# Attention scores on 32-row tiles of TensorE, the mask of the exponentials on GpSimd, and the last two batches out of the loop

## The reference, cut to what matters

```python
k = (x @ Wk).reshape(b, t, h, s)          # b, t, h, s = 8, 512, 16, 8
q = (x @ Wq).reshape(b, t, h, s)
v = (x @ Wv).reshape(b, t, h, s)
k = _layernorm(k, kln_w, kln_b)
q = _layernorm(q, qln_w, qln_b)
dot = jnp.einsum('bqhs,bkhs->bhqk', q, k) * scale
dot = jnp.where(causal, dot, -jnp.inf)
attn = jax.nn.softmax(dot, axis=-1)
out = jnp.einsum('bhqk,bkhs->bqhs', attn, v).reshape(b, t, e)
return out @ Wo + bo
```

## Time and profile before

| | |
|---|---|
| three executions, us | 1347.28, 1348.21, 1350.85; median 1348.21 |
| profiled execution | 1348.36 us, its span 1346.3 us |
| mean granted TensorE clock | 0.907 of full speed |
| busy share of the span | PE 78%, weight loads 53%, DVE 65%, ACT 44%, POOL 31% |
| chain that ended last | PE 40%, DVE 17%, issue 12% |

### The profile page before, as it was taken

One profiled execution on the slowest core, in us unless ns is written; L12 is line 12 of the kernel. 1 busy time (PEld: TensorE's weight loads), 2 busy tenths in 40 slices (PEclk: granted clock), 3 DMA queues, 4 the chain that ended last, 5 costly groups with the idle time before them and its releaser, 6 DMA issues.

```text
span 1346.3 us, 22600 instructions
## 1 busy us (share of the span) xinstructions
PE 1055.1 (78%) x6332; PEld 711.3 (53%) x6332; DVE 871.3 (65%) x1881; ACT 594.5 (44%) x1109; POOL 417.8 (31%) x460
## 2 busy tenths in 40 slices
PE   7699999879898989989898778877776321499970
PEld 4355544765555656656565454444444321399960
DVE  6677741247686777778677647999996555244445
ACT  6555554125464555555465555454454101144420
POOL 4100000771412124031000023355352177266660
PEclk9899999989998999999899989899998555699995
DMA  4011113321000000000000195000001011223206
GB/s 116 32 63 62 62 62 125 128 84 25 17 25 16 19 19 23 17 17 24 18 22 19 33 156 134 1 0 0 0 0 31 6 52 34 68 79 89 96 27 186
DMA packets 64911, 66.80 MB, mean 50 GB/s; under 512 B 7842, under 2 KB 53356, under 8 KB 62800
## 3 DMA queue, kind: packets, MB, share of 16 engines
q1 hardware_dynamic: 50256, 54.52, 14.9%
q0 software_dynamic: 4608, 6.61, 1.6%
q10 hardware_dynamic: 9984, 4.80, 1.3%
HBM read 29.90 MB, written 29.43 MB: 44 GB/s over the span
## 4 chain that ended last, share of the span: by engine, by line
PE 40%; DVE 17%; issue 12%; ACT 3%; POOL 2%; DMA 2%; DVEq 1%; POOLq 0%; ACTq 0%; SPq 0%
PE banks L1739 6%; PE banks L1753 6%; PE banks L1767 6%; PE banks L1799 5%; PE banks L2000 5%; PE banks L1992 4%; DVE D_gun L1123 2%; PE banks L1741 2%; DVE D_dmx L1079 2%; POOL rows_dram L776 2%; DVE B_mneg L951 1%; DVE D_sc L1110 1%; DMA F_back<-y_dram 1%; PE banks L1840 1%; ACT B_ot L1435 1%
## 5 line engine op out<-in xcount | busy, mean ns | idle before, releaser
L951 DVE TENSOR_REDUCE B_mneg<-banks 128x2 f32<-128x256 f32 (+3 forms) x273 | 223.9, 822 | 110.3 <-PE banks L1741 104.0
L1429 ACT ACTIVATE B_pt<-banks 128x1024 f32<-128x1024 f32 (+3 forms) x260 | 181.6, 708 | 146.2 <-PE banks L1753 144.8
L1739 PE MATMUL banks<-B_kp,B_qt 128*128 128x128 f32 (+3 forms) x546 | 181.4, 393 | 4.2 <-DMA B_kp<-B_kt 2.3
L1753 PE MATMUL banks<-B_qt,B_kp 128*128 128x512 f32 (+3 forms) x520 | 146.3, 363 | 13.3 <-issue 7.7
L1739 PEld LDWEIGHTS banks<-B_kp,B_qt 128*128 128x128 f32 x546 | 109.4, 201 | 62.9 <-ACT B_pt L1429 43.7
L1741 PE MATMUL banks<-B_mask_q,B_identb 128*128 128x128 bf16 x546 | 125.1, 234 | 0.0
L793 POOL DMA_INDIRECT y_dram<-F_yo,F_ide x80 | 80.7, 1009 | 67.0 <-DVE F_yo L1277 42.9
L1767 PE MATMUL banks<-B_pt,B_vp 128*32 128x512 f32 (+3 forms) x1024 | 98.3, 456 | 0.0
L1505 ACT ACTIVATE D_pr<-banks,D_dmx 128x512 f32<-128x512 f32 x69 | 47.5, 688 | 106.8 <-DVE D_dmx L1079 106.8
L1563 ACT ACTIVATE F_gh<-banks 128x512 f32<-128x512 f32 (+1 forms) x96 | 50.0, 527 | 100.5 <-PE banks L1992 96.1
L967 DVE SCALAR_TENSOR_TENSOR B_pt<-B_pt,B_mask_k 128x512 f32<-128x512 f32 x129 | 93.0, 721 | 1.6 <-DVE st L998 1.0
(11 more groups left out here) (275 smaller groups left out, 2240.7 us busy)
## 6 DMA issues: line engine op xcount, KB each, us to landing
B_kp<-B_kt SPq DMA_DIRECT2D x144, 64.0 KB, 2.0
comb_dram<-C_comb SPq DMA_DIRECT2D x8, 1024.0 KB, 3.8
C_cst<-comb_dram SPq DMA_DIRECT2D x8, 1024.0 KB, 4.8
rows_dram<-D_zeros SPq DMA_DIRECT2D x8, 645.0 KB, 17.1
F_xe<-rows_dram SPq DMA_DIRECT2D x8, 645.0 KB, 4.1
C_w<-w_in SPq DMA_DIRECT2D x16, 256.0 KB, 2.8
y_dram<-D_zeros SPq DMA_DIRECT2D x2, 2048.0 KB, 17.8
F_gw<-mw_in SPq DMA_DIRECT2D x16, 256.0 KB, 3.1
```

Source lines behind the costliest of these rows:

```text
L951: v.tensor_reduce(mneg[:, g % 2, qt, 2 * hp:2 * hp + 2], banks2[pair_of_banks(item)][:, :, 0:(qt + 1) * P], X, ALU.max, negate=True).then_ ...
L1429: a.activation(pt[:, 2 * hp:2 * hp + 2, PT_AT[kt]:PT_AT[kt] + w], banks2[pair_of_banks(item)][:, :, 0:w], ACT.Exp).then_inc(B_ex, 1)
L1739: t_.matmul(dst, qt1[:, g % 2, qt * P:(qt + 1) * P], kp[:, g % NG, 2 * hp + h, 0:(qt + 1) * P], start=True, stop=False)
L1753: ins = t_.matmul(dst, kp[:, g % NG, 2 * hp + h, kt * P:(kt + 1) * P], qt2[:, g % 2, kt * P:T], start=True, stop=True)
```

## The change

- **Scores.** A head's product reads only its own 32 rows of `qt1`, `qt2` and `kt_`, the two heads of an item in two different 32-row parts, each into its own bank. `kp`, its clearing, its DMAs and the waits for them go; `kt_` has four buffers, not two, and is freed by the group's last k item. In a q item both heads' products come first, then both masks.
- **Mask of the exponentials.** An affine select on GpSimd over 4 x 128 columns, in place.
- **GpSimd** walks the common list: new items nk, nq (5 steps each), nv, nb for its other work, spread over the round, and m. The wait for `C_os` now stands before all of them.
- **Times.** pv 16.3 to 16.9, O 23.2 to 23.9, A 24.0 to 25.0, AHEAD 16.2 to 16.5.
- **Peeling.** `Fori(0, B // 2 - 1)` and one more round after it in straight code, on all engines, without the early items of a round that doesn't come. `Rounds.place` and `value` count accordingly.

```diff
-    def place_before(self, stream, item, step, first):
+    def place_before(self, stream, item, step, first, last=False):
...
-        if n >= step:
-            return names[n - step], False
+        here = [x for x in names[n % step:n:step] if not (last and x in self.early)]
+        if here:
+            return here[-1], False
         return names[-1 - (len(names) - 1 - n) % step], True
...
-AHEAD = 16.2
+AHEAD = 16.5
...
         for kt in range(NT):
             yield 8 * g + 2 * kt + 14.9, ("m", g, kt)
-            yield 8 * g + 2 * kt + 16.3, ("pv", g, kt)
+            yield 8 * g + 2 * kt + 16.9, ("pv", g, kt)
         yield 8 * g - 11.2, ("K", g, 0)
         yield 8 * g - 4.8, ("Q", g, 0)
         yield 8 * g + 9.6, ("Z", g, 0)
-        yield 8 * g + 22.4 + 16.3 - 15.5, ("O", g, 0)
+        yield 8 * g + 23.9, ("O", g, 0)
         if g % NG == NG - 1:
-            yield 8 * g + 24.0, ("A", g, 0)
+            yield 8 * g + 25.0, ("A", g, 0)
             yield 8 * g + 28.0, ("W", g, 0)
+    for b in range(PG // NG):
+        for n in range(5):
+            yield 8 * NG * b - 29.3 + 1.6 * n, ("nk", b, n)
+            yield 8 * NG * b - 21.3 + 1.6 * n, ("nq", b, n)
+        yield 8 * NG * b - 13.1, ("nv", b, 0)
+        yield 8 * NG * b - 11.1, ("nb", b, 0)
...
-        kp = Bm("kp", [P, NG, G, T], F32R)
-        kt_ = Bm("kt", [P, 2, T], F32R)
+        kt_ = Bm("kt", [P, NG, T], F32R)
...
-            def spread_keys(it, first):
-                skips = [Skip(B_ROUNDS, sp, B_kp[g], f"K{g}", 64) for g in range(NG)] if first else None
-                for item in B_ROUNDS.streams["misc"]:
-                    kind, g, _ = item
-                    if kind != "K" or (first and item not in EARLY):
-                        continue
-                    sp.wait_ge(B_me, B_ROUNDS.passed("misc", it, item in EARLY, kind, g, 0))
-                    for r in range(G):
-                        rows = slice(SL * r, SL * r + SL)
-                        sp.dma_start(kp[rows, g % NG, r, :].bitcast(F32), kt_[rows, g % 2, :].bitcast(F32)
-                                     ).then_inc(B_kp[g % NG], 16)
-                    if first:
-                        skips[g % NG].after(item)
-            spread_keys(-1, True)
-            with sp.Fori(0, B // 2) as it:
-                spread_keys(it, False)
...
-            g.memset(kp[:].bitcast(F32), 0.0).then_inc(B_const, 1)
+            g.memset(vp[:].rearrange("p a t (h s) -> p (a t h) s", s=SL)[:, :, HD:HD + 1], 1.0).then_inc(B_const, 1)
...
-            with pool.Fori(0, B // 2) as hb:
-                own.loop(hb, 2 * 8)
-                for par in range(2):
-                    i0 = hb * (2 * NT) + par * NT
-                    g_last = NG * par + NG - 1 - PG
-                    for n, padded, ready in ((1, ks, B_ks), (0, qs, B_qs)):
-
-                        pool.wait_ge(B_mf, B_ROUNDS.passed("misc", hb, False, "KZ"[1 - n], g_last, 0))
+            pool.wait_ge(C_os, TILES + 4)
+
+            def pool_round(it, first, last=False):
+                skips = Skip(B_ROUNDS, pool, B_md, "m") if first else None
+
+                def masked(item):
+
+                    _, g_, kt = item
+                    pool.wait_ge(B_ex, B_ROUNDS.passed("k", it, item in EARLY, "k", g_, 2 * kt + 1))
+                    pool.sem_inc(turns, 1)
+                    w = pt[:, :, PT_AT[kt]:PT_AT[kt] + P]
+                    g.affine_select(out=w, in_=w, compare_op=ALU.is_ge, fill=0.0, base=0, pattern=[[0, G], [1, P]],
+                                    channel_multiplier=-1).then_inc(B_md, 1)
...
+                def normed(item, n, padded, ready):
+
+                    _, b, step = item
+                    ahead = item in EARLY
+                    i0 = (it + ahead) * (2 * NT) + b * NT
+                    dst = padded[:, b].rearrange("p t (h s) -> p (t h) s", s=SL)
+                    if step == 0:
+                        pool.wait_ge(B_mf, B_ROUNDS.passed("misc", it, ahead, "KZ"[1 - n], NG * b + NG - 1 - PG, 0))
...
+                    elif step < 3:
+                        own.link(g.tensor_tensor(n1[:], n1[:], (lnw, lnb)[step - 1][:, n].unsqueeze(1)
+                                                 .broadcast_to([P, NT, D]), (ALU.mult, ALU.add)[step - 1]))
...
+                for item in B_ROUNDS.order:
+                    kind, b, n = item
+                    ahead = item in EARLY
+                    if kind not in ("m", "nk", "nq", "nv", "nb") or (first and not ahead) or (last and ahead):
+                        continue
+                    if kind == "m":
+                        masked(item)
+                        if first:
+                            skips.after(item)
+                    elif kind == "nk":
+                        normed(item, 1, ks, B_ks)
+                    elif kind == "nq":
+                        normed(item, 0, qs, B_qs)
...
+            pool_round(-1, True)
+            with pool.Fori(0, B // 2 - 1) as it:
+                own.loop(it, 2 * 2 * 4)
+                pool_round(it, False)
+            own.end_loop(B // 2 - 1)
+            pool_round(B // 2 - 1, False, True)
...
-                def masked(item):
-
-                    _, g, kt = item
-                    dve.wait_ge(B_ex, B_ROUNDS.passed("k", it, item in EARLY, "k", g, 2 * kt + 1))
-                    w = pt[:, :, PT_AT[kt]:PT_AT[kt] + P]
-                    v.scalar_tensor_tensor(out=w, in0=w, scalar=BIG, in1=mask_k[:].unsqueeze(1).broadcast_to([P, G, P]),
-                                           op0=ALU.min, op1=ALU.mult).then_inc(B_md, 1)
...
-                        act.wait_ge(B_kp[(g - 2) % NG], 64 * B_ROUNDS.passed(f"K{(g - 2) % NG}", it, item in EARLY, "K", g - 2, 0))
+                        act.wait_ge(B_s2, B_ROUNDS.passed("k", it, item in EARLY, "k", g - NG, 7))
...
-                        pe.wait_ge(B_kp[g % NG], 64 * B_ROUNDS.passed(f"K{g % NG}", it, item in EARLY, "K", g, 0))
                     for h in range(2):
-                        dst = banks2[ring][:, h, 0:(qt + 1) * P]
-                        t_.matmul(dst, qt1[:, g % 2, qt * P:(qt + 1) * P], kp[:, g % NG, 2 * hp + h, 0:(qt + 1) * P],
-                                  start=True, stop=False)
+                        rows = slice(SL * (2 * hp + h), SL * (2 * hp + h) + SL)
+                        t_.matmul(banks2[ring][:, h, 0:(qt + 1) * P], qt1[rows, g % 2, qt * P:(qt + 1) * P],
+                                  kt_[rows, g % NG, 0:(qt + 1) * P], start=True, stop=False)
+                    for h in range(2):
                         ins = t_.matmul(banks2[ring][:, h, qt * P:(qt + 1) * P], identb[:], mask_q[:],
                                         start=False, stop=True)
                     ins.then_inc(B_s1, 1)
...
-                        dst = banks2[ring][:, h, 0:T - kt * P]
-                        ins = t_.matmul(dst, kp[:, g % NG, 2 * hp + h, kt * P:(kt + 1) * P], qt2[:, g % 2, kt * P:T],
-                                        start=True, stop=True)
+                        rows = slice(SL * (2 * hp + h), SL * (2 * hp + h) + SL)
+                        ins = t_.matmul(banks2[ring][:, h, 0:T - kt * P], kt_[rows, g % NG, kt * P:(kt + 1) * P],
+                                        qt2[rows, g % 2, kt * P:T], start=True, stop=True)
                     ins.then_inc(B_s2, 1)
...
-                    if first and item not in EARLY:
+                    if (first and item not in EARLY) or (last and item in EARLY):
                         continue
-                    if kind == "m":
+                    if kind in ("m", "nk", "nq", "nv", "nb"):
...
-            with pe.Fori(0, B // 2) as it:
+            with pe.Fori(0, B // 2 - 1) as it:
                 pe_round(it, False)
+            pe_round(B // 2 - 1, False, True)
```

107 lines of the change are left out of this document (49 added, 58 removed).

## The result

The changed kernel takes **1520.32 us** (median of 4 runs, 1515.56 to 1524.85), the kernel before beside it 1349.53 us (1347.28 to 1353.77). The ratio is 1.126, 95% interval 1.121 to 1.132: 171 us slower, where 24 us less was forecast.

The account below looks back on a forecast made before the run. TensorE was taken to bound stage B. The terms +9.3 -3 -2 -5 -11 -9.5 -2.5 summed to -24 us, from 1348.4 to 1325 us (forecast chance 48%), with a range of 1275 to 1372.

Parts of the forecast that it names:

- Part 1: Stage B scores on 32-row tiles: 4.1 us a group removed, 4.0 added, net -0.1, or -3 us over 29 groups.
- the drain and the open load: Added costs in Part 1: 21 more shape changes at 0.11 us (2.3) and 13 open loads at 0.11 (1.4) a group.
- Rival 3: TensorE's clock in stage B: a quarter of the stage at 1.2 GHz, +36 us, 1361 us; chance 10%.
- signs of being right: New profile: period 12.2 to 12.6 us, paired products within 0.02, `atok` idles under 1 each, first scores near 296.
- signs of being wrong: New profile: period under 11.5 or over 13.3 us, second product over 0.1 us late, or TensorE waiting for masks.
- k or q item to mask 0.1 us more than its columns: Expected in TensorE's new timeline: time from score item to mask exceeds the column time by 0.1 us.
- Rival 1: Row tiles and full array follow each other without a stop: 10.5 us a group, -58 us more, 1267 us; chance 17%.
- rival 2: Second head's load waits for the first's, +45 us, 1370; or shape changes cost 0.2 us, +55, 1380; chance 25%.
- Part 2: Mask moved to GpSimd: selection 0.7 us, cost 0; TensorE's 4.7 us of waits for VectorE's maxima drop by 2.
- Part 3: Moved items in stage B: `ot` copy wait falls 5 of 7.3 us, stall before A from 15.6 to 4.5, -11.
- Parts 4 and 5: Peeled last round: -9.5 us, one loop jump fewer -2.5; start: GpSimd waits for stage C, first scores at 296.0, +9.3.
- loop jump: Peeling stage B's last round leaves one jump fewer of three (7.7 us of "issue"): -2.5 us.

Follow-up runs that it names:

- half doses: Full-row scores with the early start, but k items alone, or q items alone, on 32-row tiles; 0.993 (k) and 0.978 (q) of the kernel before.
- e4_early_start: The changed kernel with GpSimd's wait for stage C moved from ahead of its first normalisation to the bias item; 1.125 of the kernel before.
- e7_pauses: `e6_full_early` with one 8-column product on a 32-row tile ahead of each of a group's 16 score items; 1.047 of the kernel before.
- e6_full_early: The changed kernel with scores over all 128 rows on the block diagonal and GpSimd's stage C wait moved to the bias items; 0.971 of the kernel before.
- e11_no_moves: `e6_full_early` with the order of TensorE's items put back (pv 16.3, O 23.2, A 24.0, look-ahead 16.2); 0.974 of the kernel before.
- e2_full_rows: The changed kernel with scores over all 128 rows on the block diagonal of keys, with its DMAs and waits; 0.992 of the kernel before.
- e10_junk_rows: The changed kernel with 512 useless columns on one 32-row tile ahead of each of a group's 16 score items; 1.13 and 1.17 of the kernel before.
- e3_rows64: `e2_full_rows` with each score product on the 64-row half that holds its head; 1512 and 1536 us, 1.08 to 1.10 of the kernel before.

## Why the prediction was wrong

**What bounds the kernel** stood: TensorE, and a group's length decides. The group's length as used (12.5 us) was one within a batch; the mean was 14.3, which changed no term but hid how much a batch's end costs.

**Part 1 is the step that failed**, in the clock and not in its prices. Its terms, "Net -0.1 us a group", were all taken at 2.4 GHz, and the sum had no term for the clock. Measured is +6.1 us a group, 190 us in the stage, because TensorE ran at 1.2 GHz through nearly all of it. The terms themselves hold: two products of a pair run side by side, so the second head is free; the drain and the open load were 0.32 us a visit in place of 0.36.

What row tiles would give at full clock can be bounded only. The useless columns on 32 rows show one order at both levels, 22.74 and 13.49 us, so between 5.8 us (less all 3.4 of useless columns) and 9.25 us of a group double at half clock; taken from the changed kernel's 19.43 us within a batch that is 10.2 to 13.6 us at full. The half doses come closer: 12.57 and 12.32 us where full rows take 12.36 add up to 12.5 for both. From that goes what the two places a group save where a q item directly follows a k item (a visit of 0.32 us each, and the columns that stream beside others), so an estimate is 11.6 to 12.5. The forecast's 12.4 lies in it: at full clock row tiles would have gained little or nothing, and they never ran at that clock.

**Rival 3 named the mechanism** and was mis-sized. It read "a quarter of the stage runs at 1.2 GHz" and 5 us of a group doubling, 0.25x5x29 = 36 us. Measured: nearly all of the stage (0.50 to 0.64 in every window from 320 us to 920), and 6.1 us a group net, 190 us in 31 groups. The factor of four is the share, and for it the forecast had no row: it weighed dips in the clock of the kernel before, which came with stalls, and gave this rival 10%. That the clock can stay low while the engine is busy no row of before showed; `e4_early_start` does, with 100.74 of 102 us busy at 0.50. The range ended at 1372, some 150 us short.

**Signs.** Two of the prediction's signs of being right came true: second products started within 0.02 us, and the idle time before `atok` was under 1 us each. Of its signs of being wrong one came, a period over 13.3 us. "k or q item to mask 0.1 us more than its columns" was 0.21.

The Trainium skill, TensorE: Matmul & The Clock Gate, Part 3, has tiles of different row groups start about 4 ns apart; the trace agrees (3 to 4 ns). The Trainium skill, TensorEngine Tiling (Array Packing), Key Properties, has a change of tiling mode drain the array; the runs agree for row tilings too, with the 0.09 us by the tiny products of `e7_pauses`.

**Rivals 1 and 2** did not come. Rival 1 needs changes of shape that cost nothing; they cost 0.09 us each with a tiny product. Its period of 10.5 us can't be tested at half clock. Against rival 2, the second head is free, and no change of shape cost 0.2.

**Part 2.** GpSimd's selection over 4x128 took 0.63 us, forecast 0.7, and TensorE's weight loads waited 1.5 us for masks in all, its products 0.3. "Cost 0" was right. That the waits for maxima drop by 2 us was wrong (6.2 us of waits in `e6_full_early` where 4.7 were); A's wait fell by 8 us without the moves.

**Part 3.** The waits fell as forecast (15.6 to 3.3 for A, 7.3 to 1.9 for `ot`, in `e6_full_early`), and the time did not: the moves themselves are worth 2 us of the 16, by `e11_no_moves`. The step that failed is to count a wait that disappears as time gained, on an engine whose other groups then grow.

**Not in the sum**: both products before both masks, -8.6 us. Its saving, the exposed load between heads of a q item, was counted in part 1 as if only row tiles brought it.

**Parts 4 and 5.** Queries' transposes began at 295.76 us and the first scores came at 298.79, forecast 296.0 (two items of transposes, Q and the next K, and a copy lie between, at half clock), and the first copy 10.3 us later in `e2_full_rows`, forecast 9.3; the early start takes that away. Of the 35.8 us between first and last copy 10.9 are the peeled end, forecast 9.5, 2 are the moves and 8.6 the masks' order. The 14 us that are left are the loop jump and the masks on GpSimd, forecast 2.5 + 2, with the 8 of A's wait. They were not run apart.

**What stays open.** Why the clock stands at one level or the other with the same order (`e10_junk_rows` at 660 us, `e3_rows64`) is not settled. Shown is that with all scores on row tiles the clock stays low for nearly the whole stage, that neither pauses nor the idle start do this alone, that enough full-row work lifts it, and that half the dose keeps most of the high clock. Whether it is the few rows as such, or rows and changes of shape together, is not shown.

## What to carry to other kernels

Before TensorE's work is cut into 32-row tiles, ask at which clock it will run: here the prices were nearly right at full clock, and the kernel lost 13% because the clock halved while the engine looked fully busy. Try half of the change first, and read the granted clock beside the busy share. A wait taken from the list is time only when the whole stage gets shorter: measure first to last copy, not the wait.

## What the runs showed that was not expected

- With 32-row tiles, an engine busy 57 to 60 us of 60 ran at 0.50 to 0.64 of the clock; the same kernel with full rows at 0.96 to 1.00 (`e2_full_rows`).
- At the start of the stage the clock falls in the kernel before too, for 7 us; with row tiles the same fall lasted 102 us (`e4_early_start`).
- Useless work shortened a stage: 8192 more full-row columns a group, last copy 45 us earlier.
- The same instructions ran a group in 22.7 us and, 340 us later, in 13.5 us (`e10_junk_rows`).
- Two products and then two masks, with full rows, save 0.36 us a group against the alternating order.
